# Reading the row maxima and the softmax reciprocals before the low half on VectorE, in a three-stage decoder kernel

## The reference

```python
q = (query @ Wq + bq).reshape(B, L, NKV, G, HDIM)          # 32 heads of 128, 8 key/value heads
k_, v_ = jnp.split(kv @ Wkv + bkv, 2, axis=-1)
scores = jnp.einsum('blkgd,bmkd->bkglm', q, k) * scale      # 256 queries x 1601 keys for each head
attn = jax.nn.softmax(scores, axis=-1)
o = jnp.einsum('bkglm,bmkd->blkgd', attn, v).reshape(B, L, NHEAD * HDIM)
return o @ Wo + bo
```

## Time and profile before

| | |
|---|---|
| median of three runs | 2835.67 us |
| profiled execution | 2839.65 us, span 2837.9 us |
| TensorE matmuls busy | 2676.9 us (94%) |
| TensorE weight loads busy | 2485.6 us (88%) |
| VectorE busy | 2079.8 us (73%) |
| ScalarE busy | 1913.6 us (67%) |
| GpSimd busy | 1683.3 us (59%) |
| mean granted TensorE clock | 0.986 |

### The profile page before, as it was taken

One profiled execution on the slowest core, in us unless ns is written; L12 is line 12 of the kernel. 1 busy time (PEld: TensorE's weight loads), 2 busy tenths in 40 slices (PEclk: granted clock), 3 DMA queues, 4 the chain that ended last, 5 costly groups with the idle time before them and its releaser, 6 DMA issues.

```text
span 2837.9 us, 60429 instructions
## 1 busy us (share of the span) xinstructions
PE 2676.9 (94%) x20528; PEld 2485.6 (88%) x20528; DVE 2079.8 (73%) x4144; ACT 1913.6 (67%) x4094; POOL 1683.3 (59%) x1738
## 2 busy tenths in 40 slices
PE   7899999999889999999888999999988999999997
PEld 5789989898669999999867999999976899999995
DVE  4377777778547878787854878787775587878785
ACT  4477676668447777776754877777765577767674
POOL 4389898957405656565731656566662265656563
PEclk9999999999999999999999999999999999999998
DMA  6356465613411212131331212122132121313111
GB/s 216 127 175 230 161 218 176 205 64 102 154 38 46 98 53 98 46 105 46 113 128 45 75 66 79 66 71 79 62 137 87 55 89 46 105 46 103 48 51 62
DMA packets 89999, 281.69 MB, mean 99 GB/s; under 512 B 9056, under 2 KB 9184, under 8 KB 86624
## 3 DMA queue, kind: packets, MB, share of 16 engines
q1 hardware_dynamic: 89696, 277.82, 28.4%
HBM read 233.75 MB, written 44.04 MB: 98 GB/s over the span
## 4 chain that ended last, share of the span: by engine, by line
PE 67%; issue 11%; ACT 7%; DVE 7%; POOL 7%; DMA 1%; DVEq 0%; ACTq 0%; POOLq 0%; SPq 0%
PE bank L1192 39%; PE dn L1192 14%; PE sp L1192 10%; POOL kept_s L568 3%; ACT ph L801 2%; DVE sua L1126 2%; ACT sp L806 2%; PE bank L1304 1%; PE sp L1435 1%; PE sp L1514 1%; POOL orw L587 1%; ACT kept_s L783 1%; DVE mcol L1107 1%; POOL ol L591 1%; DVE pl L1118 1%
## 5 line engine op out<-in xcount | busy, mean ns | idle before, releaser
L568 POOL TENSOR_TENSOR kept_s<-kept_s,mrow 128x512 f32<-128x512 f32 (+1 forms) x896 | 1067.4, 1223 | 456.4 <-ACT mrow L791 456.4
L1118 DVE TENSOR_TENSOR pl<-sp,ph 128x512 fp32r<-128x512 f32 (+1 forms) x896 | 578.2, 645 | 64.8 <-ACT sp L806 60.6
L801 ACT ACTIVATE ph<-kept_s 128x512 fp32r<-128x512 f32 (+1 forms) x896 | 534.3, 596 | 52.0 <-POOL kept_s L568 42.3
L806 ACT ACTIVATE sp<-kept_s 128x512 f32<-128x512 f32 (+1 forms) x896 | 506.4, 565 | 4.9 <-DVE sua L1126 4.9
L1192 PE MATMUL dn<-ph,vh 128*128 128x256 f32 (+1 forms) x1664 | 492.9, 296 | 12.5 <-ACT orw L816 8.6
L1192 PE MATMUL dn<-ph,vl 128*128 128x256 f32 (+1 forms) x1664 | 471.4, 283 | 0.0
L1192 PE MATMUL dn<-pl,vh 128*128 128x256 f32 (+1 forms) x1664 | 471.1, 283 | 0.0
L1126 DVE TENSOR_TENSOR sua<-sp,sua 128x512 f32<-128x512 f32 (+1 forms) x640 | 401.5, 627 | 0.0
L783 ACT ACTIVATE kept_s<-bank 128x512 f32<-128x512 f32 x384 | 228.6, 595 | 228.6 <-PE bank L1192 226.9
L783 ACT ACTIVATE kept_s<-sp 128x512 f32<-128x512 f32 x384 | 228.8, 596 | 182.7 <-PE sp L1192 179.1
L1192 PEld LDWEIGHTS dn<-ph,vh 128*128 128x128 f32 (+1 forms) x1664 | 317.3, 191 | 24.5 <-ACT orw L816 16.9
(11 more groups left out here) (161 smaller groups left out, 6599.5 us busy)
## 6 DMA issues: line engine op xcount, KB each, us to landing
wqx<-wq SPq DMA_DIRECT2D x128, 512.0 KB, 3.4
wox<-wo SPq DMA_DIRECT2D x64, 1024.0 KB, 4.9
wk<-wk SPq DMA_DIRECT2D x32, 512.0 KB, 3.3
wvx<-wv SPq DMA_DIRECT2D x16, 1024.0 KB, 5.8
craw<-in_ctx_t SPq DMA_DIRECT2D x16, 800.5 KB, 4.8
wqk<-in_ws SPq DMA_DIRECT2D x16, 513.0 KB, 4.7
raw<-in_wq_in SPq DMA_DIRECT2D x32, 256.0 KB, 4.1
wq<-hib SPq DMA_DIRECT2D x32, 256.0 KB, 2.0
```

Source lines behind the costliest of these rows:

```text
L568: nc.gpsimd.tensor_tensor(kept_s[:, n % 2, i:z, :], kept_s[:, n % 2, i:z, :], mrow[:, n % 2, :].unsqueeze(1).broadcast_to([P, z - i, S]), ...
L801: nc.scalar.activation(ph[:, k % PH, 0:cols], src, ACT.Exp, scale=XSCALE).then_inc(ph_ok, 1)
L806: nc.scalar.activation(pbank[k % 2][:, 0:cols], src, ACT.Exp, scale=XSCALE).then_inc(pr_ok, 1)
L1118: nc.vector.tensor_tensor(pl[:, k % PH, 0:cols], src, ph[:, k % PH, 0:cols], ALU.subtract).then_inc(pl_ok, 1)
```

## The change

In VectorE's loop over the slots, `row_maxima` and `row_reciprocals` move from behind `normalize` and `low_and_sum` of their slot to ahead of both. No instruction is added or removed, and the queues of the other engines stay as they are.

```diff
                 for g in SLOTS:
                     for j in JOBS.get(g - 1, ()):
                         job_low(*j)
+                    for h in head_of(g, MAX_COL):
+                        row_maxima(h)
+                    for h in head_of(g, SUM_ROW):
+                        row_reciprocals(h)
                     for h in head_of(g, HEAD_DIV):
                         normalize(h)
                     for h, s in slot_of(g, LOW):
                         low_and_sum(h, s)
-                    for h in head_of(g, MAX_COL):
-                        row_maxima(h)
-                    for h in head_of(g, SUM_ROW):
-                        row_reciprocals(h)
                     for h, s in slot_of(g, SCORE):
                         if s:
                             maximum(h, s)
```

## The result

| | before | after |
|---|---|---|
| median of runs, same comparison | 2837.32 us (2835.39 to 2839.72, 4 runs) | 2804.27 us (2797.68 to 2809.65, 4 runs) |
| ratio after/before, 95% interval | | 0.9877 (0.9863 to 0.9891) |
| profiled execution, span | 2839.65, 2837.9 us | 2809.65, 2807.9 us |

A forecast was written before the change was run, and what follows sets the result against it. TensorE was taken as the bound in cross-attention, idle mainly on two VectorE results. Regular heads 25.4, row starts 3.6, row ends 6.8 and first row 5.3 sum to 41 us, giving 2795 us, range 2784 to 2815.

The forecast's parts named there:

- What bounds the kernel: Cross-attention: TensorE is the bound; its remaining idle is mostly waits for VectorE's maxima (33.6 us) and reciprocals (20.3 us).
- The maxima: Light heads: reduction ahead of two VectorE instructions removes TensorE's 0.47 us wait; 4.96 us per regular batch row.
- the two smaller terms: Maxima gains forecast for the middle light head, 0.30 us, and the last light head, 0.47 us.
- The reciprocal: Moved 1.2 us sooner, it ends TensorE's waits of 0.59 us (first light head) and 0.39 us (behind V heads).
- regular stretches: Regular heads of batch rows two to four: maxima 4.96 plus reciprocals 3.5, together 8.5 us per row, 25.4 in all.
- Row starts: First two heads of batch rows two to four: 1.2 us gained each row, 3.6 us in all.
- Row ends: Last head of each row: shift 1.2 us sooner, `normalize`'s 0.59 us wait gone; 1.7 us each, 6.8 in all.
- First row: First batch row, light heads behind GpSimd: a third of 5.8 + 3.5 us, plus 1.8 us later; together 5.3 us.
- VectorE gives it back: Three light heads: VectorE lacks idle time, TensorE stops at scores or V product; 2817 or 2808 us, chance 15%.
- The fold is caught by GpSimd: VectorE's fold of the maxima (L1100) stretched by 0.99 us; 18 us off the gain, 2813 us, chance 5%.
- The turn holds VectorE: VectorE's queue stands at the reduction until the turn, 0.63 us in each of 128 heads; 2875 us, chance 4%.

The follow-up runs named there:

- the second trace of the change: The changed kernel run once more, unchanged, as reference for later kernels: median 2805.84 us, ratio to before 0.9877 (0.9861 to 0.9894).

## Why the prediction was right, and where not

**What bounds the kernel: right.** The waits for `mcol` and `rs` went, 52 us of idle time, and the kernel is 34.9 us faster; moving the reduction the other way cost 44. In the lists 12.4 us came back at the turn and 8.9 at the scores.

**The maxima: right in sum, the two smaller terms swapped.** The first light head gains 0.47 from the maxima, as forecast (the kernel with the maxima alone). Middle and last light head together measured 0.55 + 0.29 = 0.84 against 0.30 + 0.47 = 0.77. What holds TensorE is what the prediction named, the second `mxa` of the middle head. VectorE after, and PEld behind it:

```profile
1212.04 0.41 DVE L1107 TENSOR_REDUCE mcol<-sp 128x2 f32<-128x256 f32 x1
...
1215.36 0.68 DVE L1097 TENSOR_TENSOR mxa<-bank,mxa 128x512 f32<-128x512 f32 x1
```
```profile
1216.11 0.19 PEld L1192 LDWEIGHTS bank<-qh,kh 128*128 128x128 f32 x1 [0.30 <-ACT kept_s L783]
```

`mxa` ends at 1216.04 and the scores follow at 1216.11, after 0.30 us of idle time (1228.89 and 1228.96 before). It is put down to ScalarE's copy; the cause is read from the end of `mxa`. This wait falls into the interval of the last light head, hence the swap of 0.55 and 0.29.

**The reciprocal: half right, and the step that failed.** Behind the V heads 0.41 measured against 0.39. In the first light head the prediction said "The fold of the maxima behind it keeps its time, and TensorE's turn, now 0.59 sooner, still comes after it." The fold did end before the turn (1195.72 against 1196.60), but the prediction checked the turn against one of its two semaphores. The other, `normalize`, ends at 1208.53 in the trace before, and the turn's weight load starts at 1208.65, 0.12 us later. It takes the same 0.12 us where the turn visibly waits (1196.45 to 1196.57). So there was no slack at all, and of the 0.59 only what `normalize` itself comes sooner could pass: 0.20 with the reciprocal moved alone, and nothing on top of the 0.47 of the maxima. That is 4 x 0.59 = 2.4 us per row, and the regular stretches miss 8.5 - 6.4 = 2.1 each.

**Row starts: too much, 0.53 each in place of 1.2.** PEld before:

```profile
883.96 0.19 PEld L1514 LDWEIGHTS sp<-cst,rs 128*128 128x128 f32 x2 [0.60 <-DVE rs L1133]
...
886.17 0.20 PEld L1427 LDWEIGHTS sp<-cst,mxa 128*128 128x128 f32 x2 [0.56 <-issue]
```

and after:

```profile
877.75 0.20 PEld L1427 LDWEIGHTS sp<-cst,mxa 128*128 128x128 f32 x2 [1.10 <-DVE mxa L1100]
```

0.60 + 0.56 became 1.10 at the turn. The view names the fold, L1100, but that had ended at 876.90. The one that ends last is `normalize` again, VectorE after:

```profile
877.23 0.41 DVE L1140 TENSOR_TENSOR orw<-sp,orw 128x256 f32<-128x256 f32 x1
```

It ends at 877.64 and the turn's weights start 0.11 us later, as in the light head (1196.45 and 1196.57). The 0.56 us before was the same guard: `normalize` started at 885.65 there and ended at 886.06, 0.11 us ahead of the turn. It stood in the trace under the name "issue". But the guard is not what costs the time at this place. With `normalize` first the turn comes 0.37 us sooner and the fourth spread does not (0.65 against 0.68). Each half of the change alone gains 0.66 or 0.67 there, as much as both. What ends last is VectorE's queue, of which `normalize` is one instruction: before the change it has only 0.66 us of gaps in 25 us there. The prediction had named this, "since it works without a gap there", and sized it too small: of 1.7 us of waits it let 1.2 reach the end.

**Row ends: the number nearly right, by two terms that the prediction did not have.** Up to the last spread of a row the gain is 1.45, where the reduction's 1.2 was expected. VectorE's fold in the last head, before:

```profile
1394.11 1.04 DVE L1100 TENSOR_TENSOR mxa<-mxa 128x256 f32<-128x256 f32 x1
```

VectorE and GpSimd after, the same place:

```profile
1379.24 0.47 DVE L1100 TENSOR_TENSOR mxa<-mxa 128x256 f32<-128x256 f32 x1
...
1381.16 0.41 DVE L1107 TENSOR_REDUCE mcol<-sp 128x2 f32<-128x256 f32 x1
```
```profile
1381.75 0.74 POOL L591 TENSOR_TENSOR ol<-orw,oh 128x256 fp32r<-128x256 f32 x1
1382.55 1.30 POOL L568 TENSOR_TENSOR kept_s<-kept_s,mrow 128x512 f32<-128x512 f32 x1
```

The fold in the last head of each row took 1.03 to 1.04 us before and 0.45 to 0.48 after; that is 0.57 us of the 1.45 in the row shown. That was luck: nobody had forecast it. In the kernel with the turn late everywhere this fold takes 1.06 us again, and the row ends of rows two to four gain 0.86. The turn waits 0.88 us there in place of 0.40, again 0.12 us behind a `normalize` (1379.63 + 0.41 = 1380.04, turn 1380.16), but this costs nothing, as the reduction follows `sua` without a gap. GpSimd's idle 1.41 us ahead of the shift is gone; the maxima row (ready at 1382.47) and GpSimd's own work before it (1382.49) now arrive together. The 0.59 us that `normalize` waits for the reciprocal's spread lie behind the last spread, so the 1.45 do not hold them: that wait is 0.12 after, and `normalize` stands 8.24 us behind the spread in place of 8.73, 0.49 more, in rows one, two and four. The part thus came to about 1.9 at that point, against 1.7. What of it reaches the next row is not seen in the scatter between the rows.

**First row: not shown.** With its end it gained 3.7 us in one trace and 7.1 in the other, against 5.3 + 1.7 = 7.0; without the end 2.3 and 5.7 against 5.3. The two traces of one kernel differ by more than the term is in doubt. The working has a slip, too: a third of 5.8 + 3.5 is 3.1 and not 3.5.

**Rivals.** *VectorE gives it back* did not come in the regular heads, where the scores' waits stay at 0.3 us in four heads of a row; at the row starts it did, and cost about 2 us in all beyond what was allowed for. *The fold is caught by GpSimd* did not come as feared. Its durations after (min/median/max in ns, from when to when):

```profile
L1100 DVE TENSOR_TENSOR mxa<-mxa x128: 424/426/1419, 129.4 to 2751.4; 128x256 f32<-128x256 f32 x128
```

12 of 128 are shown over 0.6 us, against 13 before, but not in the same heads: the last heads of the rows left the group. The event is real, only rare in the change: it struck one regular head in the second trace of the change (0.84 us) and ten of twelve first light heads in the kernel with the maxima later. *The turn holds VectorE* started from 0.30 us in V heads; what VectorE waits for the turn is in the view of `mcol`'s operations after:

```profile
  PE sp L1427: 0.4, 2
```

Two heads, 0.4 us in all. The margin that made this rival unlikely was read correctly.

## What to carry to other kernels

When a wait is removed, the engine's next instructions run sooner too, and each has all of its semaphores to pass: for every one within the gain's length, list each wait in the code (guards of shared buffers with them, not only the data) and its slack in the trace. A slack smaller than the gain is a wait that will replace the one removed. A buffer guard may be out of sight, or stand under another name, as long as the engine comes no earlier than the guard opens; the constant 0.12 us from the end of one instruction to the start of the other gave it away here. Where the other engine has no gaps, moving a guard gains nothing. A move that frees a step in one kind of slot can cost in another, so it is tried where the slot has room and not everywhere.

## What the runs showed of the hardware

**The granted clock in the stretches between the rows.** Windows of before and after (from:to, length, then busy us of PE, PEld, DVE, ACT, POOL with their instructions, granted clock as a share of full, DMA share, GB/s); before:

```profile
1500.00:1525.00 25.00, 20.88 (x143) 14.52 (x144) 10.72 (x23) 8.36 (x18) 3.51 (x3) 1.00 0.14 43
```

after:

```profile
1483.00:1508.00 25.00, 21.35 (x129) 13.36 (x130) 10.23 (x21) 7.50 (x17) 2.50 (x2) 0.86 0.14 43
```

The granted clock of these 25 us is 0.86 after and 1.00 (2.4 GHz) before, for the same kind of work: after, it stood at 0.50 (1.2 GHz) from 1484.9 to 1491.7. In the second trace of the change it is 1.00 there. The stretch from row two's last spread to row three's first is 155.42 us after, 153.11 before and 152.58 in the second trace of the change. The regular stretches of the two traces of the change agree within 0.1 us in two rows of three. Of the 7.8 us between their spans 5.5 lie between the rows and 3.4 in the first row. That the clock causes the former is not shown beyond this one stretch. A difference of 2 us between kernels is seen in the trace's regular stretches, not in the median.

**When the two-input fold is long.** All 12 folds over 0.6 us in the trace after, and all 13 before, end 0.28 to 0.29 us behind the end of a GpSimd instruction that reads SBUF and was running, or began within a few hundredths of a microsecond, when the fold began. In the last heads of the rows before, the shift in question ended about 0.75 us into the fold, and the fold took 1.03. Where no GpSimd instruction ran at its start (65 folds after), it took at most 0.43 us. So it is a matter of when the fold starts, and a change of order moves it into this state or out of it.

**One wait, two releasers.** PEld gave "issue" for the 0.61 us of the turn, PE gave VectorE's L1140 for the same instruction. Where one track says "issue", the other is to be read.
